# Masked attention on one core: late weights in four buffers, and another split of the mask transposes

## The reference

```python
h = jnp.maximum(_layernorm(x, axis=-1), 0.0)
h1, h2 = h @ a[:256], h @ a[256:]
e = leaky_relu(h1 + h2.T, 0.01)
attention = softmax(where(adj > 0, e, -9e15), axis=1)
x + attention @ h
```

## Time and profile before

| | |
|---|---|
| median of 3 runs | 1597.63 us (1597.43 to 1597.91) |
| profiled execution | 1598.51 us, span 1596.6 us |
| TensorE, VectorE, ScalarE, POOL busy | 98%, 93%, 75%, 24% |
| mask transposes on TensorE | 624, mean 274 ns, overlapping |
| mask transposes on VectorE | 168 of two row tiles, 64 of one |
| HBM | 207 GB/s over the span |

### The profile page before, as it was taken

One profiled execution on the slowest core, in us unless ns is written; L12 is line 12 of the kernel. 1 busy time (PEld: TensorE's weight loads), 2 busy tenths in 40 slices (PEclk: granted clock), 3 DMA queues, 4 the chain that ended last, 5 costly groups with the idle time before them and its releaser, 6 DMA issues.

```text
span 1596.6 us, 41402 instructions
## 1 busy us (share of the span) xinstructions
PE 1563.8 (98%) x12950; PEld 1547.3 (97%) x12950; DVE 1490.5 (93%) x2236; ACT 1189.5 (75%) x1240; POOL 382.8 (24%) x487
## 2 busy tenths in 40 slices
PE   5999999999999999999999999999999999999999
PEld 5899999999999999999999999999999999999998
DVE  7899999999999999999999999999999999999998
ACT  7788887777877777767867767767876876876864
POOL 6264234433544321200300400400400400300300
PEclk9999999999999999999999999999999999999999
DMA  6666768777788778867767767767767866766863
GB/s 208 212 195 226 217 201 238 242 237 235 217 246 235 228 223 238 204 188 207 201 188 210 203 187 207 205 186 208 210 184 207 213 184 200 220 183 200 223 176 102
DMA packets 338829, 331.07 MB, mean 207 GB/s; under 512 B 23488, under 2 KB 245696, under 8 KB 338752
## 3 DMA queue, kind: packets, MB, share of 16 engines
q1 hardware_dynamic: 313696, 288.96, 64.0%
q10 hardware_dynamic: 25056, 41.13, 7.7%
HBM read 308.90 MB, written 21.10 MB: 207 GB/s over the span
## 4 chain that ended last, share of the span: by engine, by line
PE 73%; DVE 13%; issue 5%; DMA 2%; POOL 1%; ACT 1%; DVEq 1%; ACTq 0%; POOLq 0%
PE acc L907 24%; PE acc L910 23%; PE acc L909 23%; DVE w_lo L761 7%; DVE W L751 4%; PE T L874 3%; DMA xo<-part_sums 2%; POOL stage L396 1%; DVE T L739 1%; DVE xo L726 0%; ACT w_hi L529 0%; ACT hb L460 0%; DVE adj_in L858 0%; DVEq L748 0%; ACTq L574 0%
## 5 line engine op out<-in xcount | busy, mean ns | idle before, releaser
L907 PE MATMUL acc<-h_hi,w_hi 128*128 128x258 f32 (+1 forms) x4096 | 1182.9, 289 | 14.9 <-DVE w_lo L761 9.4
L910 PE MATMUL acc<-h_hi,w_lo 128*128 128x258 f32 (+1 forms) x4096 | 1154.6, 282 | 0.0
L909 PE MATMUL acc<-h_lo,w_hi 128*128 128x256 f32 (+1 forms) x4096 | 1151.8, 281 | 0.0
L529 ACT ACTIVATE w_hi<-W 128x1024 fp32r<-128x1024 f32 x512 | 541.2, 1059 | 356.2 <-DVE W L751 354.7
L907 PEld LDWEIGHTS acc<-h_hi,w_hi 128*128 128x128 f32 x4096 | 771.8, 188 | 28.6 <-issue 16.1
L751 DVE SCALAR_TENSOR_TENSOR W<-r_rep,g_all,T 128x512 f32<-128x512 f32 (+1 forms) x1024 | 718.9, 744 | 72.6 <-DVE w_lo L761 38.9
L909 PEld LDWEIGHTS acc<-h_lo,w_hi 128*128 128x128 f32 x4096 | 778.6, 190 | 0.0
L910 PEld LDWEIGHTS acc<-h_hi,w_lo 128*128 128x128 f32 x4096 | 774.9, 189 | 0.0
L761 DVE SCALAR_TENSOR_TENSOR w_lo<-W,w_hi 128x1024 fp32r<-128x1024 f32 x512 | 655.2, 1280 | 4.3 <-ACT w_hi L529 3.1
L520 ACT ACTIVATE mask<-adj_in,mhalf 128x2048 fp8e5<-128x2048 int32 x256 | 509.7, 1991 | 8.1 <-DMA adj_in<-in_adj_dram 4.5
L405 POOL TENSOR_TENSOR xb<-xb,stage 128x256 f32<-128x256 f32 x60 | 48.5, 808 | 667.0 <-ACT hb L584 667.0
(11 more groups left out here) (68 smaller groups left out, 251.5 us busy)
## 6 DMA issues: line engine op xcount, KB each, us to landing
adj_in<-in_adj_dram SPq DMA_DIRECT2D x672, 128.0 KB, 2.7
adj_in<-in_adj_dram SPq DMA_DIRECT2D x168, 512.0 KB, 4.3
adj_in<-in_adj_dram SPq DMA_DIRECT2D x64, 768.0 KB, 5.4
adj_in<-in_adj_dram SPq DMA_DIRECT2D x24, 1024.0 KB, 6.5
adj_in<-in_adj_dram SPq DMA_DIRECT2D x256, 64.0 KB, 2.8
part_sums<-stage ACTq DMA_DIRECT2D x24, 516.0 KB, 4.1
xo<-part_sums ACTq DMA_DIRECT2D x24, 516.0 KB, 4.6
r_rep<-r_rows SPq DMA_DIRECT2D x39, 256.0 KB, 4.2
```

The source lines that it names most:

```text
L529: nc.scalar.activation(w_hi[:, k % HL, :], W[:, k % 2, :], ACT.Relu).then_inc(s_hi, 1)
L907: nc.tensor.matmul(acc[:, t, 0:WC], w_hi[:, k % HL, cols], rhs_hi, start=start and u == 0, stop=False)
L909: nc.tensor.matmul(acc[:, t, 0:D], w_hi[:, k % HL, cols], rhs_lo, start=False, stop=False)
L910: last = nc.tensor.matmul(acc[:, t, 0:WC], w_lo[:, k % LL, cols], rhs_hi, start=False, stop=stop and u == 1)
```

## The change

`MID` becomes 0 and `LATE` 3. In steps 12 to 43 TensorE transposes all four row tiles and each chunk is loaded by one request; from step 44 on TensorE transposes one row tile of four and VectorE three, and three quarters of a chunk come in turned pieces.

In the late visits `W` gets four buffers instead of two (`deep`). Their memory is one tile `halves` of eight pieces of 512 columns: pieces 0 and 1 are `hb`, 2 to 5 the old `W`, 6 and 7 `hq`. Once all of `h` is made, `hq` and half of `hb` are idle; piece 0 goes on holding `hmean` and `hshare`. Seven pieces make four buffers: those of pairs 1 and 3 of a step share piece 5. So in late visits the first instruction of `W` waits for `w_lo` of pair g-4 instead of g-2, and only the second one of the odd pairs still for that of g-2. Visit 22, the first with four buffers (`enter`), keeps the old waits in its first step, and its third pair waits until POOL has made all of `h_lo`.

```diff
-    MID, LATE = 1, 2
-    N_MID = 2 * 6
+    MID, LATE = 0, 3
+    N_MID = 2 * 22
...
-        W = sb("W", [P, 2, PAIR], f32)
+        halves = sb("halves", [P, 8, BLK], f32)
+        W = halves[:, 2:6, :].rearrange("p (k u) j -> p k (u j)", u=2)
+        deep_w = [halves[:, 2:4, :], halves[:, 4:6, :], halves[:, 6:8, :], halves[:, 1:6:4, :]]
...
-        hq = sb("hq", [P, G, D], f32)
-        hb = sb("hb", [P, G, D], f32)
+        hq = halves[:, 6:8, :].rearrange("p u (e d) -> p (u e) d", d=D)
+        hb = halves[:, 0:2, :].rearrange("p u (e d) -> p (u e) d", d=D)
...
-            def weights(V, c, c_tot, g, k, wait):
+            def weights(V, c, c_tot, g, k, wait, enter=False):
...
-                if wait:
+                if wait and (not V.deep or enter):
                     dve.wait_ge(s_lo, g - 1)
+                if enter and k == 2:
+                    dve.wait_ge(s_hl, NB)
                 for u in range(2):
                     e = 2 * (k % 2) + u
-                    last = nc.vector.scalar_tensor_tensor(W[:, k % 2, u * BLK:(u + 1) * BLK], r_rep[:, V.v % 2, :],
+                    if V.deep and not enter and u == 0:
+                        dve.wait_ge(s_lo, g - 3)
+                    if V.deep and not enter and u == 1 and k % 2 == 1:
+                        dve.wait_ge(s_lo, g - 1)
+                    out = deep_w[k][:, u, :] if V.deep else W[:, k % 2, u * BLK:(u + 1) * BLK]
+                    last = nc.vector.scalar_tensor_tensor(out, r_rep[:, V.v % 2, :],
```

More of the change, by code:

```diff
@@ L4 @@
 from collections import namedtuple
-Visit = namedtuple("Visit", "v n0 b c0 its prev pb f pa make phase made nxt head tail dt dt_next")
+Visit = namedtuple("Visit", "v n0 b c0 its prev pb f pa make phase made nxt head tail dt dt_next deep")
 def masked_graph_attention(nc, x, adj, a, out):
@@ L195, in quarter @@
             def quarter(v, q, prev, make=None, phase=None, made=None, nxt=None, head=False, turn=False,
-                        dt=MID, dt_next=MID):
+                        dt=MID, dt_next=MID, deep=False):
                 visit(Visit(v=v, n0=2 * v, b=v - SH * q, c0=Q * q, its=Q // CI, prev=prev,
@@ L200, in quarter @@
                             nxt=v + 1 - SH * q if nxt is None else nxt,
-                            head=head, tail=False, dt=dt, dt_next=dt_next))
+                            head=head, tail=False, dt=dt, dt_next=dt_next, deep=deep))
             def finals(m, prev):
@@ L230, in run @@
                 h_made()
-            quarter(22, 2, "added", dt=LATE, dt_next=LATE)
-            quarter(23, 2, "added", nxt=0, dt=LATE, dt_next=LATE)
+            quarter(22, 2, "added", dt=LATE, dt_next=LATE, deep=True)
+            quarter(23, 2, "added", nxt=0, dt=LATE, dt_next=LATE, deep=True)
             if h_summed is not None:
@@ L514, in convert @@
                     act.wait_ge(s_turn[kc], 64 * (n - N_MID + 1))
-                if dt == G:
+                if dt == G and not (isinstance(n, int) and n == N_MID):
                     act.wait_ge(s_TV, (n - N_MID) * CI + kc - 1)
@@ L522, in convert, with round_w @@
                                      ACT.Sign, bias=mhalf[:, 0:1], scale=1.0, saturate=False).then_inc(s_mask, 1)
-            def round_w(g, k, wait):
+            def round_w(g, k, wait, deep=False):
                 act.wait_ge(s_w, g + 1)
@@ L528, in round_w @@
                     act.wait_ge(s_used, g + 1 - HL)
-                nc.scalar.activation(w_hi[:, k % HL, :], W[:, k % 2, :], ACT.Relu).then_inc(s_hi, 1)
+                if deep:
+                    nc.scalar.activation(w_hi[:, k % HL, :].rearrange("p (u j) -> p u j", u=2), deep_w[k],
+                                         ACT.Relu).then_inc(s_hi, 1)
+                else:
+                    nc.scalar.activation(w_hi[:, k % HL, :], W[:, k % 2, :], ACT.Relu).then_inc(s_hi, 1)
             def evacuate(V):
@@ L671, in steps @@
                         convert(n + (kc + 1) // CI, (kc + 1) % CI, True, V.dt_next if last and kc == 1 else V.dt)
-                    round_w(n * PI + k, k, True)
+                    round_w(n * PI + k, k, True, V.deep)
                     if first:
@@ L754, in weights, with subtract @@
                 last.then_inc(s_w, 1)
-            def subtract(g, k, wait):
+            def subtract(g, k, wait, deep=False):
                 dve.wait_ge(s_hi, g + 1)
@@ L760, in subtract @@
                     dve.wait_ge(s_used, g + 1 - LL)
-                nc.vector.scalar_tensor_tensor(w_lo[:, k % LL, :], W[:, k % 2, :], 0.0, w_hi[:, k % HL, :].bitcast(f32),
-                                               ALU.max, ALU.subtract).then_inc(s_lo, 1)
+                if deep:
+                    nc.vector.scalar_tensor_tensor(w_lo[:, k % LL, :].rearrange("p (u j) -> p u j", u=2), deep_w[k], 0.0,
+                                                   w_hi[:, k % HL, :].bitcast(f32).rearrange("p (u j) -> p u j", u=2),
+                                                   ALU.max, ALU.subtract).then_inc(s_lo, 1)
+                else:
+                    nc.vector.scalar_tensor_tensor(w_lo[:, k % LL, :], W[:, k % 2, :], 0.0,
+                                                   w_hi[:, k % HL, :].bitcast(f32),
+                                                   ALU.max, ALU.subtract).then_inc(s_lo, 1)
             def denominators(V):
@@ L813, in steps @@
                     dve.wait_ge(s_rr, 16 * V.v)
+                enter = first and isinstance(V.v, int) and V.v == 22
                 for k in range(PI):
@@ L829, in steps @@
                         if not (isinstance(V.v, int) and V.v == 1 and first and k < 2):
-                            subtract(g - 2, (k + 2) % 4, True)
+                            subtract(g - 2, (k + 2) % 4, True, V.deep and not (enter and k < 2))
                         if first:
@@ L834, in steps @@
                             side_work(V, PI + k)
-                        weights(V, c + kc, n * CI + kc, g, k, True)
+                        weights(V, c + kc, n * CI + kc, g, k, True, enter)
             run(dve, steps)
             for k in range(2, 4):
-                subtract(NTOT * PI - 4 + k, k, True)
+                subtract(NTOT * PI - 4 + k, k, True, True)
             dve.wait_ge(s_xlast, 16)
```

4 lines of the change are left out of this document (2 added, 2 removed).

## The result

The changed kernel takes 1583.34 us, median of 4 runs (1582.39 to 1584.89), beside 1597.77 (4 runs) for the kernel before: ratio 0.9906, 95% interval 0.9889 to 0.9924. That is 14 us off where I had forecast 24; it lies in the range of 1566 to 1587, nearer its upper end.

What follows compares the result with a forecast made beforehand. TensorE's instruction count was taken as the bound, with some 20 us of stalls on top and VectorE bounding busy late steps. Terms: -19.0 - 7 + 7.2 - 5 = -23.8 us, giving 1574 us; range 1566 to 1587.

Steps and rivals of the forecast that it cites:

- The pace of the late stage: Late visits, TensorE: two mask transposes become one in each of 168 chunks, 19.0 us off; quiet steps at 11.65.
- The transpose and the buffers on VectorE: Late visits, VectorE: three-tile transpose about 0.59 us, +0.13 a chunk; with four buffers `W` begins about 1.13 us after `w_lo`.
- 0.42 a chunk: Late visits, VectorE: time saved because four buffers remove waits of `W` for `w_lo`, 0.20 and 0.22.
- I take 7 of the 13.8 as recovered; ends 0 and 13.8: Late stage: of 13.8 us lost against TensorE's quiet pace, 7 us would go as VectorE gains slack.
- 49.0 needed before: Four busy late steps, old kernel: VectorE's work alone needs 49.0 us, matching the 49.06 seen, so VectorE is bound there.
- Where stalls go, what is late next is TensorE itself: ScalarE term: same count and size of instructions, so only TensorE would be late next; no time booked.
- 0.113 a transpose: TensorE's price in us for one mask transpose, booked for 168 late chunks (19.0 off) and 64 middle ones (7.2 added).
- 2.58 us in four steps: Four busy late steps: extra time of VectorE's `w_lo` beside POOL's work.
- The middle stage: Steps 12 to 43: TensorE's fourth transpose adds 7.2 us, 5 of 6.3 us of stalls go; stage near 396.7 us.
- nothing is late: Transfers: late loads in shorter pieces raise DMA busy share 6%, engines 0.71 busy; exception, the first step of long visits.
- no stall goes: Rival, chance 0.16: stalls are handovers between POOL, ScalarE and VectorE, as long as before; -11.8 us, 1586.
- VectorE becomes the bound: Rival, chance 0.10: in the late stage the removed wait saves nothing and the longer transpose remains; 1597 to 1615 us.

Runs made afterwards that it cites:

- freed version: Changed kernel with a second buffer for the mean's share, so ScalarE waits for POOL's tile before the last, and the short visit's row store issued later: 1570.45 us, ratio 0.9826.

## Why the prediction was half right

*The pace of the late stage* came out as worked: 11.88 to 11.66 a step, 18.5 us over 84 steps against the 19.0 named.

*The transpose and the buffers on VectorE*: 0.59 us and `W` 1.12 after `w_lo`, both as named. The Trainium skill's rule that dropping the wait gains nothing ("VectorE: DVE Perf Modes", section "The DRAIN you can't avoid") would have made this 0; going back to two buffers cost 24 us (1583 to 1607). The same section also says that a next instruction that is not held starts earlier, which I had left out, and this is what the rows show (0.08 before the end). The wait was worth more than my 0.42 a chunk inside the loop, about 0.64, since I had measured it outside.

*The step that failed* is "I take 7 of the 13.8 as recovered; ends 0 and 13.8". It went the other way, to 17.9, beyond the end. The runs split it: the four buffers took the stall from 13.8 to 12.4 (11.1 with `MID` 0), 1.4 to 3 of the 7, and the third tile put 6.8 back. The arithmetic behind it fits VectorE (49.0 needed before; the busy steps lie outside the loop, where the short gaps hold), and the error was to let TensorE's pace be the only thing next in line: "Where stalls go, what is late next is TensorE itself". Next in line was the chain from POOL's additions over ScalarE's row scaling and mask conversion to TensorE's transpose. The busy steps keep its length, 48.68 us for four with two tiles and 48.94 with three, so that the 0.113 a transpose that I had booked for every chunk is not won there. I had also counted what POOL costs VectorE, 2.58 us in four steps, and not asked who pays when VectorE starts first. POOL does: its additions are longer with four buffers and two or three tiles on VectorE, and ScalarE queues the mask conversion behind them. That this chain is the cause and not the loads or VectorE is shown from both of its ends, by freeing ScalarE (1570.45) and by halving POOL's additions (1570.92). The freed version, at 7.6 us of late stall, stands where my sum had put the changed kernel (6.8), and its 1570.5 lies 3.5 below the forecast.

*The middle stage*: I had +7.2 - 5 = +2.2, measured -0.9. Of the stalls all 6.3 went, not 5, and the pace rose from 12.13 to 12.30 a step, 5.4 us instead of 7.2, since the four old steps that I had taken for quiet held a little waiting (the single step in the earlier trace rows takes 12.07).

*Transfers*: "nothing is late" was not so: ScalarE's waits for loads of the mask rose from 1.3 to 10.7 us in the late stage, and the share of the quiet steps rose by a fifth, not by 6%. It cost little here: the freed version has the same loads and 7.6 us of late stall.

*The sum.* For the profiled execution I had 1574.7. The late stall came out 11.1 above my 6.8 and the pace 0.5 short; the middle stage gave 3.1 more and the start of the program 0.8: 1574.7 + 11.1 + 0.5 - 3.1 - 0.8 = 1582.4, as measured. So that the time lies in the range is in part luck: the largest error was partly paid by terms that I had not foreseen.

Of the rivals, "no stall goes" (1586) was the nearest in time and right in naming the handovers between POOL, ScalarE and VectorE, but not in its terms: the late stall grew by 4.1 and the middle's went altogether; what I held against it, that VectorE's work alone explains the busy steps, was true of the kernel before and says nothing of the one after. The rival on the slower side, "VectorE becomes the bound", is what the split without the buffers does: 1607.

## What to carry to other kernels

Where two engines exclude each other at a port, the one that starts first makes the other late, and making one faster can turn that round; look for who waits for the other one, and through which in-order queue, before booking the gain. A cost that repeats hundreds of times is to be read inside the loop that repeats it, from a grouped view, not from one stretch that happens to lie outside it. A price per instruction read from quiet steps holds only where that engine is the bound: in the busy steps, which kept their length, TensorE's saved transposes bought nothing. And when two engines are level, a shift of work between them and the removal of a wait must be judged together: here the buffers alone were worth 3 us, the split alone lost 9, and both won 14.

## What the hardware showed that was not expected

A VectorE instruction that waits for the one just before it began 0.10 to 0.14 us behind its end in the steps outside the inner loop of the eight-step visits, and 0.22 to 0.25 inside it (158 and 160 places in the late stage of the kernel before). Why the loop makes a difference was not tried; most of the outer steps lie in a loop too, that over the passes. Without the wait it began 0.07 to 0.09 before that end.

Where `w_lo` and one of POOL's additions met, the one that had started first kept its length. POOL's addition ended 0.5 to 0.6 us behind the end of a `w_lo` that was ahead of it (1.80 instead of 0.74 at worst), and `w_lo` 1.1 us behind the end of an addition that was ahead of it (1.72 instead of 1.20).

Loading three row tiles of four in requests of 32 partitions raised the busy share of the DMA engines from 0.69 to 0.84 at 202 GB/s in quiet steps, and pieces four times as long brought it only to 0.80.
